# A first modulation in two halves by feature, a gate spread by 32-row groups, and the load of the gate's modulation ahead of the second x

## The reference

```
mod = (silu(c) @ wmod).reshape(2, 6, 1, 512)          # wmod: 512 x 3072
sa, ca, ga, sb, cb, gb = the six vectors of each batch
ga, gb = (2 * (g >= 0) - 1) * maximum(abs(g), 0.25)
h = layernorm(x) * (1 + ca) + sa
x = x + ga * (h @ (weight where its 32x32 block of mask has any 1).T + bias)
h = layernorm(x) * (1 + cb) + sb
x = x + gb * lora_ffn(h)     # silu(h w1) * (h w3), then w2; hidden 1376; each w has a rank-16 pair
```

## Time and profile before

| | us |
|---|---|
| median of three runs | 253.67 (253.4 to 253.71) |
| the profiled execution | 253.31 |
| its span in the trace | 251.5 |
| busy in the span: PE, DVE, POOL, ACT | 244.5, 134.3, 96.8, 90.0 |
| granted clock of PE, mean | 0.996 of full speed |

### The profile page before, as it was taken

The page is one execution under the profiler, slowest core; times in us unless marked ns, Lnnn a source line. Parts: engine busy times, 40 slices in busy tenths (PEclk is TensorE's granted clock), DMA queues, the critical chain, the costliest instruction groups (busy, mean ns, idle before and its releaser), DMA issues.

```text
span 251.5 us, 3398 instructions
## 1 busy us (share of the span) xinstructions
PE 244.5 (97%) x1202; PEld 193.4 (77%) x1202; DVE 134.3 (53%) x215; ACT 90.0 (36%) x152; POOL 96.8 (38%) x102
## 2 busy tenths in 40 slices
PE   7999999998999999999999999999999999999993
PEld 6757876886888888888888778888888888888772
DVE  3568599899899854654654631741233123312224
ACT  2358563843423465465432412122212221222110
POOL 1329792326423130330310360497356335633300
PEclk9999999999999999999999999999999999999998
DMA  6999990022324413313317630040000000000005
GB/s 187 385 367 408 414 384 21 3 86 83 83 83 126 128 42 122 85 46 116 92 46 106 44 19 0 12 154 0 3 1 0 0 0 3 0 0 0 3 1 168
DMA packets 12529, 24.02 MB, mean 96 GB/s; under 512 B 1240, under 2 KB 2648, under 8 KB 12512
## 3 DMA queue, kind: packets, MB, share of 16 engines
q1 hardware_dynamic: 12352, 23.65, 30.2%
q10 hardware_dynamic: 160, 0.15, 0.3%
HBM read 21.18 MB, written 2.10 MB: 93 GB/s over the span
## 4 chain that ended last, share of the span: by engine, by line
PE 88%; DMA 4%; DVE 2%; POOL 1%; SPq 1%; issue 1%; ACT 1%; DVEq 0%; POOLq 0%; ACTq 0%
PE up_b L1114 24%; PE up_a L1114 24%; PE acc L1128 8%; PE acc L1129 8%; PE acc L1127 8%; DMA wa<-in_weight 4%; PE acc L1064 4%; PE side L1095 2%; POOL ht_lo L399 1%; DVE xt L806 1%; PE side L1099 1%; PE side L1064 1%; PE acc L967 1%; PE up_a L991 1%; PE acc L1027 1%
## 5 line engine op out<-in xcount | busy, mean ns | idle before, releaser
L904 DVE TENSOR_TENSOR g<-up_b,g 128x512 f32<-128x512 f32 (+1 forms) x22 | 15.2, 690 | 64.5 <-PE up_b L1114 64.5
L1128 PE MATMUL acc<-w_lo,g_hi 128*128 128x512 f32 (+1 forms) x88 | 34.7, 394 | 0.0
L1129 PE MATMUL acc<-w_hi,g_lo 128*128 128x512 f32 (+1 forms) x88 | 34.7, 394 | 0.0
L1127 PE MATMUL acc<-w_hi,g_hi 128*128 128x512 f32 (+1 forms) x88 | 34.6, 394 | 0.0
L654 ACT ACTIVATE g<-up_a 128x512 f32<-128x512 f32 (+1 forms) x22 | 13.1, 597 | 58.8 <-PE up_a L1114 58.8
L794 DVE SCALAR_TENSOR_TENSOR raw<-side,raw 128x512 f32<-128x512 f32 (+2 forms) x33 | 21.5, 677 | 22.9 <-PE side L1095 16.3
L661 ACT ACTIVATE g_hi<-g 128x512 fp32r<-128x512 f32 (+1 forms) x22 | 13.9, 633 | 49.1 <-DVE g L904 49.1
L442 POOL TENSOR_TENSOR w_lo<-work,w_hi 128x512 fp32r<-128x512 f32 (+1 forms) x11 | 14.2, 1287 | 41.3 <-ACT w_hi L580 41.3
L573 ACT ACTIVATE w_hi<-raw 128x512 fp32r<-128x512 f32 (+2 forms) x33 | 20.3, 627 | 21.7 <-DVE raw L794 21.6
L908 DVE TENSOR_TENSOR g_lo<-g,g_hi 128x512 fp32r<-128x512 f32 (+1 forms) x22 | 22.7, 1033 | 8.7 <-ACT g_hi L661 8.4
L1114 PE MATMUL up_a<-ht_hi,w_lo 128*128 128x512 f32 (+1 forms) x88 | 24.2, 396 | 1.1 <-DVE w_lo L800 1.1
(11 more groups left out here) (161 smaller groups left out, 381.5 us busy)
## 6 DMA issues: line engine op xcount, KB each, us to landing
raw<-in_ffn SPq DMA_DIRECT2D x33, 256.0 KB, 2.7
wmod_sb<-in_wmod SPq DMA_DIRECT2D x4, 1024.0 KB, 11.5
xt<-in_x SPq DMA_DIRECT2D x8, 256.0 KB, 8.2
wmod_sb<-in_wmod SPq DMA_DIRECT2D x1, 2048.0 KB, 15.7
out<-xt SPq DMA_DIRECT2D x8, 256.0 KB, 2.5
mask_sb<-in_mask SPq DMA_DIRECT2D x4, 256.0 KB, 9.8
wa<-in_weight SPq DMA_DIRECT2D x4, 256.0 KB, 9.9
lora_raw<-in_lora SPq DMA_DIRECT2D x1, 512.0 KB, 10.4
```

What stands on the lines that cost most here:

```text
L904: nc.vector.tensor_tensor(g[0:w], up_b[0:w], g[0:w], ALU.mult).then_inc(g_ready, 1)
L1127: nc.tensor.matmul(acc[t][:], hi, down_hi[j][0:w], start=(j == 0), stop=False)
L1128: nc.tensor.matmul(acc[t][:], hi, down_lo[j][0:w], start=False, stop=False)
L1129: last = nc.tensor.matmul(acc[t][:], lo, down_hi[j][0:w], start=False, stop=(j == HT - 1))
```

## The change

- The first modulation is made in two halves by feature (`mod_products(0, f)`, `first_columns(f)`): the host orders wmod so that half f has shift and scale of feature blocks 2f and 2f + 1, 128 columns in each of four row groups, and each half is loaded by a transfer of its own. The first half feeds `high` and `whole` of blocks 0 and 1, the second, made between the first attend products, those of blocks 2 and 3. The second modulation uses the new order of wmod with products of 128 columns too.
- SP: mask 0 ahead of the modulation's first half; weight 0, mask and weight 1 ahead of its second; the gate's modulation ahead of the second x.
- PE: turn 3, the second half, and mask blocks 2 and 3 go later, between attend products; the spread goes ahead of `attend(0, 3, 0)`. It is one step of eight products, each with the 32 rows of its own group, and group q writes bank q.
- The copies of the spread gate, one for each bank and 2 x 128 columns, are DVE's and not ACT's. ACT makes three of batch 1's four norms and not two. `lora_part(1)` moves on DVE to behind the second modulation's columns, `lora_high(1)` on ACT to behind `high(7)`. POOL makes the first root of batch 1 ahead of `masked_weight_low(3)`. `bias_high`, `bias_part` and `mask_sum(0)` go earlier. There are two more warm matmuls, and the three fill products after the turns are gone.

The diff without some changes of names and counts, in which `...` marks what is left out and each piece is set to the left by the same amount:

```diff
...
-WARM_MATMULS = 26
+WARM_MATMULS = 28
...
-GATE_COPIES = B
+GATE_COPIES = T
+CENTRED = {0: 2, 1: 2, 4: 4, 5: 4, 6: 6, 8: 8, 9: 8, 10: 10}
+NORMS_ACT = (2, 5, 8)
+NORMS_DVE = (2, 3, 4)
...
-wmod_a_loaded = [sem(f"wmod_a_loaded{h}") for h in range(2)]
+wmod_a_loaded = [sem(f"wmod_a_loaded{f}") for f in range(2)]
...
 def mask_bank(k):
...
-def mod_bank(second):
-    return up_a if second else up_b
+def mod_out_at(second, f):
+    if second:
+        return up_a[:, f * P:(f + 1) * P]
+    return acc[0][:, 2 * P:3 * P] if f else up_b[:, 0:P]
+def cols_at(second, f):
+    if second:
+        return up_a[:, HALF + f * P:HALF + (f + 1) * P]
+    return acc[0][:, 3 * P:4 * P] if f else up_a[:, 0:P]
+def mods_done(q):
+    i, k = divmod(q, KT)
+    return 3 if PASSES[i][1] else 1 + k // 2
 def merge_bank(r):
...
-    def load_mod(lo, hi, loaded, ks=slice(0, KT)):
-        sp.dma_start(wmod_sb[:, ks, lo * D:hi * D], wmod_rows[:, ks, lo * D:hi * D]).then_inc(loaded, 16)
+    def load_mod(lo, hi, loaded):
+        sp.dma_start(wmod_sb[:, :, lo * D:hi * D], wmod_rows[:, :, lo * D:hi * D]).then_inc(loaded, 16)
+    def load_first_mod(f):
+        at = slice(f * D, (f + 1) * D)
+        sp.dma_start(wmod_sb[:, :, at], wmod_rows[:, :, at]).then_inc(wmod_a_loaded[f], 16)
     load_x(0)
-    load_mod(SHIFT_A, GATE_A, wmod_a_loaded[0], slice(0, KT // 2))
     sp.dma_start(mask_sb[:, 0], mask[:, 0]).then_inc(mask_loaded[0], 16)
-    load_mod(SHIFT_A, GATE_A, wmod_a_loaded[1], slice(KT // 2, KT))
+    load_first_mod(0)
     sp.dma_start(wa[:, 0], weight[:, 0]).then_inc(wa_loaded[0], 16)
-    for k in range(1, KT):
-        load_attention(k)
+    load_attention(1)
+    load_first_mod(1)
+    load_attention(2)
+    load_attention(3)
+    load_mod(GATE_A, SHIFT_F, wmod_ga_loaded)
     load_x(1)
-    load_mod(GATE_A, SHIFT_F, wmod_ga_loaded)
     for n in range(LORA_FIRST):
...
+    root(T, 2)
...
-    root(T, 2)
...
-    def mod_evacuate(second):
-        act.wait_ge(mod_out, 1 + second)
-        nc.scalar.activation(mod_rows[:, second], mod_bank(second)[:, 0:HALF], ACT.Copy
+    def first_mod_evacuate(f):
+        act.wait_ge(mod_out, 1 + f)
+        nc.scalar.activation(mod_rows[:, 0, f * P:(f + 1) * P], mod_out_at(0, f), ACT.Copy
...
+    def mod_evacuate():
+        act.wait_ge(mod_out, 3)
+        nc.scalar.activation(mod_rows[:, 1], up_a[:, 0:HALF], ACT.Copy).then_inc(mod_rows_ready, 1)
     def norm(n):
...
-        act.wait_ge(centre_ready, 8 if n == 2 * T + 2 else 2 * i + 2)
+        act.wait_ge(centre_ready, CENTRED[n])
...
-    def gate_copy(b):
-        act.wait_ge(spread_out, b + 1)
-        act.wait_ge(block_on_ready, KT)
-        nc.scalar.activation(gate_row_a[b], acc[2 + b][:], ACT.Copy).then_inc(gate_row_ready, 1)
     def lora_high(n):
...
+    bias_high()
...
-    bias_high()
-    mod_evacuate(0)
+    first_mod_evacuate(0)
...
+    first_mod_evacuate(1)
...
+    norm(T)
...
-    norm(T)
...
-    for n in range(LORA_FIRST):
-        lora_high(n)
-    gate_copy(0)
-    gate_copy(1)
+    norm(T + 2)
+    lora_high(0)
...
-    for n in range(LORA_FIRST, len(LORA_CUTS)):
+    for n in range(1, len(LORA_CUTS)):
...
-    mod_evacuate(1)
+    mod_evacuate()
...
-        dve.wait_ge(cols_ready, 1 + second)
+        dve.wait_ge(cols_ready, mods_done(q))
...
-    def columns(second):
-        dve.wait_ge(cols_out, 1 + second)
-        src = up_a[:, second * HALF:(second + 1) * HALF].rearrange("p (c v h b) -> p v h c b", c=2, v=2, h=2)
-        nc.vector.tensor_copy(shift[:, second].rearrange("p (h c) b -> p h c b", h=2), src[:, 0, :, :, 0:B])
-        nc.vector.tensor_scalar(one_plus[:, second].rearrange("p (h c) b -> p h c b", h=2),
+    def first_columns(f):
+        dve.wait_ge(cols_out, 1 + f)
+        src = cols_at(0, f).rearrange("p (v c b) -> p v c b", v=2, c=2)
+        ks = slice(2 * f, 2 * f + 2)
+        nc.vector.tensor_copy(shift[:, 0, ks], src[:, 0, :, 0:B])
+        nc.vector.tensor_scalar(one_plus[:, 0, ks], src[:, 1, :, 0:B], 1.0, None, ALU.add
+                                ).then_inc(cols_ready, 1)
+    def columns():
+        dve.wait_ge(cols_out, 3)
+        src = up_a[:, HALF:2 * HALF].rearrange("p (f v c b) -> p v f c b", f=2, v=2, c=2)
+        nc.vector.tensor_copy(shift[:, 1].rearrange("p (f c) b -> p f c b", f=2), src[:, 0, :, :, 0:B])
+        nc.vector.tensor_scalar(one_plus[:, 1].rearrange("p (f c) b -> p f c b", f=2),
...
     def mask_sum(k):
...
+    def gate_copy(q):
+        dve.wait_ge(spread_out, 1)
+        dve.wait_ge(block_on_ready, KT)
+        src = acc[q][:, 2 * P:(2 + B) * P].rearrange("p (b n) -> p b n", b=B)
+        nc.vector.tensor_copy(mask_sb[:, 0:B, q * P:(q + 1) * P].bitcast(F32), src
+                             ).then_inc(gate_row_ready, 1)
     def lora_part(n):
...
     def attn_gate(n):
...
-        dve.wait_ge(gate_row_ready, b + 1)
+        dve.wait_ge(gate_row_ready, GATE_COPIES)
...
     nc.vector.tensor_copy(half_on[:], const[:, HALF_ON:HALF_ON + 2]).then_inc(half_on_ready, 1)
+    bias_part()
+    mask_sum(0)
     norm(2)
     norm(3)
-    mask_sum(0)
     mask_on(0)
-    bias_part()
     mask_weight(0)
+    first_columns(0)
     mask_sum(1)
     mask_on(1)
-    columns(0)
     mask_weight(1)
...
     mask_on(2)
+    first_columns(1)
+    mask_weight(2)
     mask_sum(3)
-    mask_weight(2)
     mask_on(3)
...
     moment(6)
+    centres(T)
     moment(7)
-    centres(T)
     gates_of(0)
-    norm(T + 2)
+    centres(T + 2)
     norm(T + 3)
-    for n in range(LORA_FIRST):
-        lora_part(n)
+    for q in TURN_BANKS:
+        gate_copy(q)
+    lora_part(0)
     whole(4)
...
-    columns(1)
+    columns()
+    lora_part(1)
...
-        pe.wait_ge(normed_by_act, (2, 4, 7)[i])
-        pe.wait_ge(normed, (2, 4, 5)[i])
+        pe.wait_ge(normed_by_act, NORMS_ACT[i])
+        pe.wait_ge(normed, NORMS_DVE[i])
         if i == 1:
-            pe.wait_ge(h_ready, (2, 1, 3, 4)[k])
-            if k == 1:
-                pe.wait_ge(gates_ready, 1)
-            elif k > 1:
-                pe.wait_ge(gate_row_ready, k - 1)
+            pe.wait_ge(gate_row_ready, k + 1)
         elif i == 2 and k == 0:
             pe.wait_ge(attn_gated, T)
-            pe.wait_ge(cols_ready, 2)
+            pe.wait_ge(cols_ready, 3)
         elif i == 2 and k == 1:
...
     def turn_tile(t):
...
-        pe.wait_ge(normed, 5 + t + 1)
+        pe.wait_ge(normed, NORMS_DVE[-1] + t + 1)
...
-    def mod_rows_part(second, ks):
-        for k in ks:
-            if second:
-                pe.wait_ge(wmod_f_loaded, 16)
-                pe.wait_ge(attn_gated, 1)
-            else:
-                pe.wait_ge(wmod_a_loaded[k // 2], 16)
+    def mod_products(second, f):
+        if second:
+            pe.wait_ge(wmod_f_loaded, 16)
+            pe.wait_ge(attn_gated, 1)
+        else:
+            pe.wait_ge(wmod_a_loaded[f], 16)
+            if f:
+                pe.wait_ge(*h_done(0))
+        dst = mod_out_at(second, f)
+        for k in range(KT):
...
-                at = ((SHIFT_A, SCALE_A), (SHIFT_F, SCALE_F))[second][q // 2] * D + q % 2 * HALF
-                last = nc.tensor.matmul(mod_bank(second)[q * QUAD:(q + 1) * QUAD, 0:HALF], silu_c[:, k],
-                                        wmod_sb[:, k, at:at + HALF], start=(k == 0), stop=(k == KT - 1))
-        if KT - 1 in ks:
+                at = (SHIFT_F * D if second else 0) + f * D + q * P
+                last = nc.tensor.matmul(dst[q * QUAD:(q + 1) * QUAD], silu_c[:, k],
+                                        wmod_sb[:, k, at:at + P], start=(k == 0), stop=(k == KT - 1))
+        if f or not second:
...
-    def columns(second):
-        pe.wait_ge(mod_rows_ready, 1 + second)
-        for c in range(2):
-            at = second * HALF + c * P
-            last = nc.tensor.transpose(up_a[:, at:at + P], mod_rows[:, second, c * P:(c + 1) * P], ident)
+    def first_columns(f):
+        pe.wait_ge(mod_rows_ready, 1 + f)
+        nc.tensor.transpose(cols_at(0, f), mod_rows[:, 0, f * P:(f + 1) * P], ident).then_inc(cols_out, 1)
+    def columns():
+        pe.wait_ge(mod_rows_ready, 3)
+        for f in range(2):
+            last = nc.tensor.transpose(cols_at(1, f), mod_rows[:, 1, f * P:(f + 1) * P], ident)
...
     def gate_rows(n):
...
-    def gate_spread(b):
+    def gate_spread():
...
-        pe.wait_ge(h_ready, 3 + b)
-        for q in range(KT):
-            row = q * QUAD + b
-            last = nc.tensor.matmul(acc[2 + b][:, q * P:(q + 1) * P], ident[:, row:row + 1].broadcast_to([P, P]),
-                                    gates_a[:], start=True, stop=True)
+        pe.wait_ge(cols_ready, 2)
+        pe.wait_ge(h_ready, KT)
+        for b in range(B):
+            for q in range(KT):
+                rows = slice(q * QUAD, (q + 1) * QUAD)
+                row = q * QUAD + b
+                last = nc.tensor.matmul(acc[q][:, (2 + b) * P:(3 + b) * P],
```

(42 more changed lines are left out.)

## The result

The changed kernel is slower: 256.50 us (median of 4, 255.59 to 256.62) against 253.69 (253.40 to 253.91) beside it, a ratio of 1.0104 with an interval of 1.0078 to 1.0129. The forecast was 253.0 in a range of 252.0 to 254.3. The profiled execution took 256.62, its span is 254.8 (253.31 and 251.5 before).

The account below looks back on a forecast made before the run. PE and DVE were taken as tied at 34.7 us; -0.95 (front) + 0.1 (second modulation) + 0.2 (`lora_part(1)`) = -0.65 us from the profiled 253.31, 252.66, put at 253.0 for the runs' median, range 252.0 to 254.3.

Parts of the forecast that it names:

- What bounds the kernel: Bias products of batch 1: PE and DVE tied at 34.7 us, so a gain of PE alone is worth nothing.
- Part 1: The start: `high(0)` at about 13.1, PE attending from about 15.3, 2.1 us earlier, and at the spread at 26.7.
- Part 2: Second x behind the gate's load: second tile at 23.6, last root of x1 done at 28.0 against 28.91 before.
- the bound of 28.6: Late end for x1's last root, from the second x tile landing with most of the delay ahead of it.
- the bound of 24.2: Late end for the second x tile's landing behind the gate's load, with most of the delay ahead of it.
- the -0.95: Front term of the sum: 0.95 us gained at 34.7, on PE and DVE alike.
- Part 3: Gates at 27.8, spread 0.5 to 0.7 us, four copies 1.5 us, third `whole` done at 33.75: 0.95 us gained.
- Part 4: Second modulation in 64 passes costs +0.1 us; moved `lora_part(1)` beside POOL's power operation costs 0 to 0.5, taken as 0.2.
- The 292 ns row: Evidence against a wait at `lora_part(1)`: DVE's two-input gate operation kept its time inside POOL's power operation.
- The clock: Sign of a wrong forecast: a granted clock below 1.00 after PE's new idle times, with no size given.
- The slower one: Rival, chance 0.16: the second x is late, over 0.5 us slower; 254.9 if its tile lands at 25.4.
- Given back: Rival, chance 0.16: DVE, full from 50 to 60 us, loses the 0.95 to `lora_part(1)` and a longer root: 253.5.

Follow-up runs that it names:

- e3: The changed kernel with `centres` made by two one-column operations, each with one tensor input and `rstd` as per-partition scalar: 254.06 us, 1.0015 of the kernel before.
- e12: e3 with `lora_part(1)` taken off DVE, its product made by ACT and its sum by POOL: 253.50 us against 253.54, 1.0002.
- e5: The changed kernel with POOL's first root of batch 1 again behind `masked_weight_low(3)`, `centres` keeping two inputs: 255.04 us, 1.0052 of the kernel before.
- e4: The changed kernel with x loaded ahead of the gate, one-input `centres` and four fill products together: 254.07 us, 1.0025 of the kernel before.
- e1: The changed kernel with the second x loaded ahead of the gate's modulation again: 255.01 us, 1.0060 of the kernel before.
- e2: The changed kernel with twelve fill products on PE ahead of the spread: 255.44 us, 1.0076 of the kernel before.
- e10: e8 with `lora_part(0)` on DVE ahead of `whole(4)` and POOL's `spread(0)` ahead of `low(KT)`: 253.18 us against 253.54 for the kernel before, 0.9982.
- e6: The kernel before with only `lora_part(1)` moved, to between `columns` and `centres` of the third pass: 254.20 us against 253.56, 1.0022.
- e11: e10 with `lora_part(1)` off DVE, its product made by ACT and its sum by POOL: 252.72 us, 0.9966 of the kernel before.
- e7: The changed kernel with x first, one-input `centres`, earlier moments and roots, POOL held until the norm is done, `lora_part(0)` and `low(KT)` moved: 256.10 us, 1.0107.
- e8: e7 with six fill products on PE, all moments ahead of `centres(T)` and gates ahead of `centres(T + 2)`: 255.54 us, 1.0079 of the kernel before.

## Why the prediction was wrong, point by point

**What bounds the kernel: right.** PE and DVE were tied at 34.7, and a gain of PE alone was worth nothing. e3 and e12 show that in full.

**Part 1: right.** `high(0)` came at 13.15 (13.1 forecast), the first attend product at 15.03 (15.3), and PE was through with the products ahead of the spread at 27.1 (26.7).

**Part 2: this is the step that failed.** It put the last deviations at 28.0; they were done at 29.44 + 0.71 = 30.15, beyond the bound of 28.6 and beyond the 28.91 of before. Two terms make it up, 1.1 and 1.0 us.
- The first root started at 25.76, not at 24.65, since the second tile's moments started at 24.71 and not at 23.6. Two things stood in the way, either of them enough. The tile landed at about 24.6 (issued at 12.4, 12.2 to landing), beyond the bound of 24.2. And DVE, which I had let be free, was held by `mask_weight(3)` until 23.5, since that operation took 1.18 beside POOL; the second tile's moments could not have started before 24.3. Before the change the first moments started at 21.80; the change had moved `mask_blocks(3)` back on PE and with it `mask_weight(3)` on DVE, and the forecast gave it no place there. In e3 and e5, with the same order of loads, the second tile landed at 23.3 and 23.7, and its moments still started at 24.4; in e4, with x first, too. So an x that is in time gives 0.3 here, and the rest is DVE. (The lower bound for the tile, 22.9 "by bytes alone", was also too early: it landed at 20.6 before, and 1 MB at 407 GB/s adds 2.6.)
- "The last tile's moments, queued on DVE behind `centres(T)` (25.9), end at 26.8 and are just not late." They were queued behind an instruction that I had costed at 0.16 and that took 1.14; they started at 28.01. I had looked at the 160 ns row of `centres`, taken with POOL idle, and had asked only of the big operations what POOL does beside them. Without this term (e3) the root is done at 28.94.

By the rule of the Trainium skill (SBUF — State Buffer, Who interferes with whom), a VectorE instruction with two SBUF inputs and a GpSimd one that reads SBUF exclude each other, and "Issue order, not op shape, decides who blocks." The trace agrees: 1.14, 1.15 and 1.17 beside POOL, 0.16 with POOL idle (e5), 0.33 for two of one input (e3). It does not agree where POOL's own operation has two columns (last section), and there the measurement decides. I weighed that rule at `lora_part(1)` and the norm, where I already had rows, and not at the new neighbour that POOL's changed order gave `centres`.

In the terms of the sum: of the -0.95 nothing came even with `centres` mended (e3); `centres`, for which it had no term, cost 2.3; `lora_part(1)` cost 0.6 for 0.2; and the second modulation, +0.1, cost nothing that a run shows. That is some 2.8 lost where 0.65 was to be gained.

**Part 3: half right.** The gates were done at 29.78 and not at 27.8, by the same waits. The copies came as forecast (0.41 each, 1.40 for the four against 1.5). The spread by row groups takes 0.72 where PE is at 2.4 GHz (e1, e2, e10), at the edge of the 0.5 to 0.7; in the changed kernel 1.24, at 1.2 GHz. The norm's wait was forecast, but `centres(T + 2)` took its place: it was issued first, waited 1.15, and the norm then ran in 0.53. In e3 the norm waits, 1.25. That the gain of 0.95 hung on the last root is right in kind: with the root at 28.94 (e3) the third `whole` is done at 34.68, and with the moments moved ahead (e10) at 34.04.

**Part 4: right for the modulation, too small for `lora_part(1)`.** The 64 passes took 1.88, against 1.86. `lora_part(1)` measured 0.6, where I took 0.2 and a bound of 0.5. I had priced only the power operation; POOL's two-column addition ahead of it was the one that waited in e6 (0.78 for 0.23), in e3 it was the power operation (1.04 for 0.71). The 292 ns row was a poor witness: it shows that a meeting with the power operation can pass unharmed, not that it does.

**The clock: listed and not priced.** "A granted clock below 1.00 after PE's new idle times" stood among the signs of a wrong forecast, with no price in the range. It cost 0.9 us of the 2.8. The forecast itself had PE idle for about 1 us before the spread, and e3 kept its clock over 1.39; the 2.7 us came with the delay on DVE. The Trainium skill (TensorE: Matmul & The Clock Gate, Part 1) says that the array runs at half clock unless recent activity has released it. The trace agrees: the granted clock is 0.50 from 29.0 on, with PE without work since 27.1, and 1.00 again from 35.8, with PE at work from 29.83 on.

**The rivals.** The slower one named a late second x, and 254.9. The side was right, and x was late as it feared (second tile at about 24.6), but that was not what cost the time: in e4, against e3, the order of the loads is worth nothing. That the side came out right is luck. "Given back" by way of `lora_part(1)` did occur, for 0.6.

## What to carry to other kernels

An operation of two columns that shares VectorE's and GpSimd's port is priced by its neighbour, not by its size: when the order of either engine changes, list what now stands beside each two-input operation, the smallest too, and write the small ones with a per-partition scalar instead of a second tensor. That freed an operation of one column (e3); the norm of 512 columns, written with two such scalars, still waited for POOL (1.25 for 0.53), so what is large needs another place. An engine that is brought forward to wait longer may come out of the wait at half clock, so cover the wait or move the work behind it as well. And a front that is tied between two engines pays only when both move: PE's two microseconds were worth nothing alone (e12), and 0.8 us with the order of DVE and POOL rewritten around them (e11).

## What the runs showed of the hardware

- No one length of idle time told whether the clock would fall. It held after 1.39 us (e3) and after 1.99 us (e1); it fell within the 2.72 us of the changed kernel, and after 1.64 (e7) and 1.84 (e5) about 0.9 and 1.2 us into the work that followed. Executions of one kernel differed as well: two of four in e5, three of six in e8. What decides was not isolated.
- In the meetings with a long operation the one issued second waited, whichever engine it was on. DVE's two columns took 1.15 instead of 0.16 behind POOL's subtraction, POOL's two columns 0.78 instead of 0.23 behind DVE's `lora_part(1)`. Beside POOL's two-column operations the waits were small or none: before the change `centres` took 0.16 issued at 27.96 in POOL's addition of 27.83 to 28.05, and the gate operation 0.29 to 0.32 beside its power operation, which took 0.71, but 0.85 in e5.
- The spread's sixteen passes in four row groups of 32, 128 columns each, took 0.72 where sixteen over the whole array took 1.95 in the same view (0.66 in e4 and 1.78 before along the chain of waits).
